# Cross-attention kernel: the chunk loops written out on every engine, and GpSimd's value work cut in four pieces

## The reference, cut to what matters

```python
q = _fq_sym(q, axis=-1); k = _fq_sym(k, axis=-1)
v = _fq_sym(v, axis=2)                       # one scale per head and column, over all keys
attn = jnp.einsum('bhqd,bhkd->bhqk', q, k)
attn = jax.nn.softmax(attn.astype(jnp.float32), axis=-1)
attn = _fq_unsigned(attn, axis=-1)           # rounded to multiples of max/255
out = jnp.einsum('bhqk,bhkd->bhqd', attn, v)
```

## Time and profile before

| | |
|---|---|
| median of 3 runs | 5876.34 us (5856.25 to 5903.51) |
| profiled execution | 5865.44 us, of which the span from first to last instruction is 5863.2 us |
| mean granted TensorE clock | 0.888 of full speed |
| busy share of the span | PE 90%, DVE 74%, ACT 66%, POOL 61% |
| heads 0 to 14 | 906.0 to 4834.2 us: 3928.2 us, 261.9 us a head |
| last head | from 4834.2 us, clock 0.50 throughout; its chunks 2 to 6 take 45.8 to 46.0 us each |

### The profile page before, as it was taken

How to read it: one execution, slowest core, us unless ns; L and a number is a source line. 1 busy time by engine, 2 the same in 40 slices (tenths; PEclk the granted TensorE clock), 3 DMA queues, 4 the chain that set the end, 5 groups by cost and what they waited for, 6 DMA issues and landing times. The chain is left out here.

```text
span 5863.2 us, 172761 instructions
## 1 busy us (share of the span) xinstructions
PE 5275.7 (90%) x53204; PEld 1997.3 (34%) x53204; DVE 4340.2 (74%) x7292; ACT 3874.4 (66%) x6380; POOL 3562.0 (61%) x3506
## 2 busy tenths in 40 slices
PE   5888598999999999999999999999998999978969
PEld 3444212333333333333333333333333332224535
DVE  6888698887887887787788788888887882224444
ACT  1444207887988887887889788888888885631000
POOL 2555606777877777787778677777777785630000
PEclk8999658999999999999999999999999995559979
DMA  3655301111111111111111111111111111211101
GB/s 90 182 179 182 104 17 24 31 25 26 29 30 26 26 30 26 31 24 30 26 26 28 28 28 25 31 27 29 26 29 25 31 44 63 87 36 30 32 16 29
DMA packets 242528, 265.26 MB, mean 45 GB/s; under 512 B 48397, under 2 KB 223645, under 8 KB 241946
## 3 DMA queue, kind: packets, MB, share of 16 engines
q1 hardware_dynamic: 176570, 202.39, 13.3%
q10 hardware_dynamic: 65376, 54.68, 3.0%
HBM read 173.41 MB, written 82.06 MB: 44 GB/s over the span
## 5 line engine op out<-in xcount | busy, mean ns | idle before, releaser
L914 ACT ACTIVATE e<-ps_sweep,sk 125x448 f32<-125x448 f32 x6144 | 3536.5, 631 | 763.8 <-ACTq L913 671.5
L971 DVE TENSOR_REDUCE unit_max<-ps_sweep 128x500 f32 (+1 forms) x5376 | 3261.8, 670 | 602.0 <-DVEq L970 442.1
L1117 POOL TENSOR_SCALAR r<-e 125x896 f32<-125x896 f32 x3072 | 2886.6, 953 | 1119.6 <-POOLq L1116 678.3
L721 PE MATMUL ps_sweep<-q,k 54*128 54x448 bf16 x6144 | 2085.9, 377 | 32.5 <-PEq L711 24.8
L733 PE MATMUL ps_sweep<-k,q 48*128 48x500 bf16 x5376 | 1803.9, 399 | 118.0 <-PEq L732 108.0
L755 PE MATMUL ps_av<-e,zt 126*17 126x224 f32 x24576 | 1843.4, 377 | 0.8 <-issue 0.8
L748 PE MATMUL ps_av<-r,vt 125*16 125x224 f16 x12288 | 886.8, 277 | 97.4 <-PEq L741 61.6
L733 PEld LDWEIGHTS ps_sweep<-k,q 48*128 48x128 bf16 x5376 | 370.8, 95 | 1381.6 <-issue 1363.5
L721 PEld LDWEIGHTS ps_sweep<-q,k 54*128 54x128 bf16 x6144 | 546.2, 94 | 684.2 <-issue 593.4
L755 PEld LDWEIGHTS ps_av<-e,zt 126*17 126x17 f32 x24576 | 654.9, 99 | 45.4 <-issue 39.2
L748 PEld LDWEIGHTS ps_av<-r,vt 125*16 125x16 f16 x12288 | 299.2, 86 | 934.8 <-issue 934.8
(11 more groups left out here) (184 smaller groups left out, 2678.2 us busy)
## 6 DMA issues: line engine op xcount, KB each, us to landing
k_rows<-krows ACTq DMA_DIRECT2D x48, 1000.0 KB, 6.8
k<-k_rows SPq DMA_DIRECT2D x128, 281.2 KB, 3.8
k<-k_rows SPq DMA_DIRECT2D x384, 93.8 KB
cx<-in_ctxT SPq DMA_DIRECT2D x48, 500.0 KB, 4.7
v_raw<-kv SPq DMA_DIRECT2D x24, 1000.0 KB
vr<-v_raw SPq DMA_DIRECT2D x128, 187.5 KB
cb<-in_ctxT SPq DMA_DIRECT2D x16, 1500.0 KB, 6.4
gu_w<-in_gu SPq DMA_DIRECT2D x34, 192.0 KB, 2.3
```

The source lines that it names most:

```text
L721: pe.matmul(ps2[(2 * i + g) % 3][:, 0:HALF], k2[u][:, i * KT:i * KT + P], q2[y][:, g * HALF:(g + 1) * HALF], start=True, stop=True, tile_p ...
L914: act.activation(e[i % SLOTS][0:KT, g, :], ps2[(2 * i + g) % 3][0:KT, 0:HALF], ACT.Exp, scale=sk[u][:, i:i + 1]).then_inc(e_wrote, 1)
L971: top = dve.tensor_reduce(unit_max[:, b, bass.ds(j * NPIECE + at, 1)], ps[:, 0:SB], axis=AX.X, op=ALU.max)
L1117: pool.tensor_scalar(r[i % SLOTS][:, :, :], e[i % SLOTS][0:KT, :, :], 1.0, HALFWORD, ALU.mult, ALU.add)\
```

## The change

Two things, both in `attention()`. `over_chunks` becomes a plain Python loop, so the eight chunks of a round stand in a row in the program of SP, PE, ACT and DVE, and likewise in POOL's; only the loops over heads stay. And POOL's two value instructions per chunk become four with 12 tiles' values each: scaling after tiles 1 and 4, rounding after tiles 8 and 12. `vt_ready` is signalled after each half, and PE waits for it before both of its value sums.

```diff
-    SCALED, WHOLE, SUMMED = SLOTS - 2, SLOTS + 1, (SLOTS + 7, SLOTS + 11)
+    SCALED, WHOLE, SUMMED = (1, 4), (SLOTS, SLOTS + 4), (SLOTS + 7, SLOTS + 11)
+    VTILES = CT // 2
...
-        def over_chunks(eng, chunk):
-
-            chunk(0, 0, True, False)
-            with eng.Fori(0, (NCH - 2) // 2) as jj:
-                for u in (1, 0):
-                    chunk(jj * 2 + 2 - u, u, False, False)
-            chunk(NCH - 1, 1, False, True)
+        def over_chunks(chunk):
+
+            for j in range(NCH):
+                chunk(j, j % 2, j == 0, j == NCH - 1)
...
             def sum_values(u, half):
 
 
-                if half == 0:
-                    pe.wait_ge(vt_ready, 1).then_inc(vt_ready, -1)
+                pe.wait_ge(vt_ready, 1).then_inc(vt_ready, -1)
...
-            def scaled_values(h):
-
-                pool.wait_ge(vr_ld, 16).then_inc(vr_ld, -16)
-                pool_done(pool.tensor_tensor(vr[:, :, :], vr[:, :, :],
+            def scaled_values(h, half):
+
+                if half == 0:
+                    pool.wait_ge(vr_ld, 16).then_inc(vr_ld, -16)
+                part = vr[:, half * VTILES:(half + 1) * VTILES, :]
+                pool_done(pool.tensor_tensor(part, part,
                                              v_inv[:, bass.ds(h * HDIM, HDIM)].rearrange("p (o d) -> p o d", o=1)
-                                             .to_broadcast([KT, CT, HDIM]), ALU.mult))
-
-            def whole_values(u):
-                pool.wait_ge(v_free[u], 1).then_inc(v_free[u], -1)
-                pool_done(pool.tensor_scalar(vt[u][:, :, :], vr[:, :, :], ROUND, ROUND, ALU.add, ALU.subtract))
+                                             .to_broadcast([KT, VTILES, HDIM]), ALU.mult))
+
+            def whole_values(u, half):
+                if half == 0:
+                    pool.wait_ge(v_free[u], 1).then_inc(v_free[u], -1)
+                tiles = slice(half * VTILES, (half + 1) * VTILES)
+                pool_done(pool.tensor_scalar(vt[u][:, tiles, :], vr[:, tiles, :], ROUND, ROUND, ALU.add, ALU.subtract))
                 pool.sem_inc(vt_ready, 1)
-                pool.sem_inc(vr_free, 1)
+                if half == 1:
+                    pool.sem_inc(vr_free, 1)
 
             def chunk(u, h):
 
                 for i in range(CT):
                     rounded(i)
-                    if h is not None and i == SCALED:
-                        scaled_values(h)
-                    if h is not None and i == WHOLE:
-                        whole_values(1 - u)
+                    if h is not None and i in SCALED:
+                        scaled_values(h, SCALED.index(i))
+                    if h is not None and i in WHOLE:
+                        whole_values(1 - u, WHOLE.index(i))
...
-            scaled_values(0)
-            whole_values(0)
+            for half in range(2):
+                scaled_values(0, half)
+                whole_values(0, half)
             with pool.Fori(0, HEADS - 1) as h:
-                with pool.Fori(0, (NCH - 2) // 2):
-                    for u in range(2):
-                        chunk(u, h)
-                chunk(0, h)
-                chunk(1, h + 1)
-            with pool.Fori(0, (NCH - 2) // 2):
-                for u in range(2):
-                    chunk(u, HEADS - 1)
-            chunk(0, HEADS - 1)
-            chunk(1, None)
+                for j in range(NCH):
+                    chunk(j % 2, h + j // (NCH - 1))
+            for j in range(NCH):
+                chunk(j % 2, HEADS - 1 if j < NCH - 1 else None)
```

More of the change, by code:

```diff
@@ L687, in head @@
                     sp.wait_ge(t_stored, 16 * SROWS).then_inc(t_stored, -16 * SROWS)
-                over_chunks(sp, chunk)
+                over_chunks(chunk)
             sp.dma_start(decay[:, :], bcast(t["L1_xattn_decay"], P)).then_inc(decay_landed, 16)
@@ L873, in chunk @@
                         pe.wait_ge(t_copied, 3).then_inc(t_copied, -3)
-                over_chunks(pe, chunk)
+                over_chunks(chunk)
                 if not second:
@@ L951, in head @@
                         copy_t_rows(n)
-                over_chunks(act, chunk)
+                over_chunks(chunk)
             t_wrote = semaphore("t_wrote")
@@ L1083, in chunk @@
                         weigh_context(j * 2 + 1, 1)
-                over_chunks(dve, chunk)
+                over_chunks(chunk)
             for u in range(2):
```

## The result

| | before | after |
|---|---|---|
| median | 5869.06 us (5856.25 to 5903.51) | 6187.6 us (6181.07 to 6205.99) |
| ratio | | 1.0538 [1.0487, 1.059], slower |
| span and mean granted clock of the profiled execution | 5863.2 us, 0.888 | 6185.5 us, 0.859 |

The account below looks back on a forecast made before the run. PE's instruction stream was taken to set the pace, so PE's idle time adds directly. Sum: 5865.4 - 154.5 (returns) + 328.5 (stops) + 126 (clock) + 15 (chunk 7) + 23 (last head) = 6203 us, range 5990 to 6400.

Parts of the forecast that it names:

- Part 1: Chunks in a row remove PE's long returns inside a head: chunks 2 to 5 of 15 heads save 154.5 us.
- POOL's return: POOL's longer body might make its return per head long, some 3.3 us 15 times: taken as 0, at most 50 us.
- POOL's wait and PE's stop: POOL waits for the values' load after tile 1; PE stands 3.7 us in step 7, net 3.65 a chunk, 328.5 us.
- The clock: PE's stops in chunks 1 to 6 lower its clock: 1.4 us a chunk, 126 us, between 0 and 4.9 a chunk.
- Chunk 7: Stop of 1.8 to 2.7 us at step 7, partly hidden by pieces waiting in four banks: 1.0 a head, 15 us.
- Chunk 0: Tile 3 is ready some 7.3 us after the load's issue, before POOL gets tile 5: no stall.
- The last head: Later load costs 3 us in each of chunks 2 to 6 and 8 us in chunk 1: 23 us together.
- the wait misses PE: Rival: POOL's wait does not reach PE, so the kernel gets faster, 5656 us; chance 0.07.
- it is half as long: Rival: the wait is half as long, a stall of 2 us a chunk without clock loss, 5929 us; chance 0.10.
- the clock falls as in head 3: Rival: the clock falls that far after every stop in chunks 1 to 6, 315 us more, 6518 us; chance 0.12.
- the fetches belong to the place in the code: Rival: long fetches come from the code's place, not PE's returns, so nothing is saved, 6357 us; chance 0.05.
- the fifth: Rival: POOL's return per head becomes long and is felt, 6253 us; chance 0.06.

Follow-up runs that it names:

- e7: The kernel before with the chunks written in a row on PE alone, old value work kept: 5701.8 us, ratio 0.9731.
- e9: The kernel before with the chunks written in a row on PE and DVE alone: 5679.0 us, ratio 0.9696.
- e1: The after kernel with the old value work (two instructions, after tiles 6 and 9), so only the chunks in a row: 5662.8 us, ratio 0.9668.
- e6: The after kernel with the halves of the scaling after tiles 3 and 5 in place of 1 and 4: 5846.6 us, ratio 0.9988.
- e4: The after kernel with the four value pieces after tiles 6, 8, 10 and 13, load left in place: 5660.0 us, ratio 0.9659.

## Why the prediction was right

**Part 1** was forecast at -154.5 us, all of it PE's returns. Chunks 1 to 6 gave -180.3 (2824.5 to 2644.3). PE's returns alone gave 144.8 of them (e7), 10 less than forecast. Most of the rest, 31 us by e7 and e9, is DVE's loop: its register reads, which the text took to "cost nothing with DVE idle for 3 us a chunk", and its returns, which it did not price since their record is short. That step failed. Idle time on DVE is no proof, for by the program PE needs the bank that the reduction frees, and that comes later by each read and each return. That longer programs cost nothing held: e1's chunks take 29.4 us at clock 1.00.

**POOL's return** was taken at 0, with 50 us as the other end. The branch still records 45 ns, but the sequencer's next instruction came 2.4 to 2.8 us after it at each of the 15 returns of after, and 0.2 us in before. So the rule of the Trainium skill (Runtime: NRT & Kernel Launch, section Instruction fetch mechanics) is borne out for POOL too; but PE's idle time in chunk 0 is 1.46 us against 1.57 before, so nothing was felt. The price was right; the row cannot show what it was read for, since the branch's own record doesn't hold the stop. The same goes for "no other engine's branch is long": behind the return of the loop over heads ACT and DVE stood for 2.6 to 3.2 us in both kernels, and SP for 4.5 to 4.7 in after against 0.24 in before. In e1, where SP's is as long, PE's idle time in chunks 0 and 7 is 1.62 and 2.91 us against 1.57 and 2.75, so this too was hardly felt.

**POOL's wait and PE's stop.** Forecast: 3.65 us a chunk net, of it 3.7 in step 7, which comes 11.7 us in. Measured in chunk 5 of head 2: 3.17, at 11.2; and in the mean over chunks 1 to 6 3.62 - 0.60 = 3.0 more idle time than in e1. Three terms were each a little too long: the load was issued 4.1 us into the chunk and not 4.4, from issue to multiply it took 4.1 and not 4.3, and the half multiply took 0.59, forecast 0.7. Where SP's issue was late, as in chunk 3, the stop was 5.16. The 0.45 us of step 9 and the 0.1 of the halves are not there: step 7's 3.17 us is all but 0.03 of PE's idle time in chunk 5. The 0.6 of step 15 is gone, as forecast.

**The clock** was forecast at 1.4 us a chunk. The chunk grew by 4.93 in all, so 1.9 fell to the clock and what follows it. The two errors, -0.6 and +0.5, cancel: 5.05 a chunk was forecast. That the total came so near is luck in this part. The first end of the bounds, 0, is what e6 comes near to (0.45), with stops of 1.2 us; no run had a mean near the other end, 4.9. The Trainium skill's case (TensorE: Matmul & The Clock Gate, section HAM oscillation), a clock that falls each time in a loop that waits for a DMA, agrees with the trace of after, where 90 of 90 chunks have time at 1.2 GHz; in e6, with shorter stops for the same load, 10 have.

**Chunk 7** was set at 1.0 us a head and cost 3.0: 2.3 more idle time, and the clock. The four banks' reserve of work did not hide the stop as I took it to. The forecast had the stop right, at 1.8 to 2.7 us, and took too much off for the reserve. **Chunk 0** had no stop, as forecast (the text's 7.3 us for tile 3 add up to 7.1, which changes nothing), and took 560.7 us against 563.9. But with the rows alone it took 537.2; the 23 us go with more time at 1.2 GHz (12.8 us a chunk against 8.2), for a reason not settled. **The last head** cost 20.2 us, forecast 23: its chunk 1 went from 51.6 to 59.3 (8 forecast), chunks 2 to 6 by some 2.5 each (3 forecast).

The sum: -180 + 443 + 45 - 3 + 20 - 2 (the rest) = 323 against 322 measured by the spans and 338 forecast. Part 1's 26 us more gain and chunk 7's 30 us more cost cancel too. Of the rivals, that the wait misses PE, that it is half as long, that the clock falls as in head 3, and that the fetches belong to the place in the code are all ruled out by the rows above. Of the fifth, POOL's return did become long and was not felt. The first would have been true with the first piece after tile 6 (e4), and e6, after tile 3, comes near the second.

## What to carry to other kernels

Moving work earlier on an in-order engine moves its wait earlier too: before it is moved, find when its input is issued, and what stands in that queue ahead of it. Here moving one call, so that the load is issued first, turned 1.054 into 0.960. A chunk's price is the stop plus the clock: the clock's part was 0.45 us a chunk with 2.1 us of idle time in short stops, 1.73 with 2.6 and 2.04 with 3.6 in a single one. Unrolling paid most where long returns stood on the pacing engine, PE; a short return or a register read on another engine counts where PE needs the buffer that it frees.

## What the runs showed that I had not expected

**A DMA issue stretches under code loading.** SP's issues of `k2` take 0.37 us in the median, but up to 2.28 in after and 1.73 in before. In heads 0 to 14, those over 0.9 us, 9 of 9 in before and 16 of 16 in after, overlap a transfer on the queue that loads instructions; of the shorter ones 15 of 351 and 33 of 344 do. After, by line (columns as in the earlier trace rows):

```profile
L650 SPq DMA_DIRECT2D k<-k_rows x355: 315/369/2281, 935.9 to 5099.7; - x178
```

and the timeline of SP in chunk 3 of head 2, where one of three issues took most of 3.16 us and the values' load came 6.1 us into the chunk, in place of 4.1; PE's 5.16 us above is its effect. That loading the code stretches the issue is argued from this overlap; no run tried it by itself.

```profile
1563.73 3.16 SPq L650 DMA_DIRECT2D k<-k_rows  x3
...
1568.58 0.29 SPq L662 DMA_DIRECT2D vr<-v_raw  x1
```

**A register read of 57 ns between a wait and its instruction** starts the instruction 0.09 us later, 42 times a chunk, and goes with some 0.15 us of the chunk's length, though DVE is idle for 3 us of it. **A return whose branch records 60 ns** keeps DVE idle 0.47 us longer before its first reduction, and the chunk behind it is 0.57 us longer than the reads explain.
